# A graph network on one Trainium2 core: fourteen unused products behind each macro's sums in the last layer

## The reference

```python
def _L3_gnn_ref(embeddings, edge_src, edge_dst, edge_val, W1, b1, W2, b2):
    ego_emb = embeddings @ W1.T + b1
    messages = edge_val[:, None] * embeddings[edge_src]
    neighbor_emb = jax.ops.segment_sum(messages, edge_dst, num_segments=embeddings.shape[0])
    interaction_emb = neighbor_emb * embeddings
    side_emb = (neighbor_emb + interaction_emb) @ W2.T + b2
    out = ego_emb + side_emb
    out = jnp.where(out >= 0, out, LEAKY_SLOPE * out)
    norm = jnp.sqrt(jnp.sum(out * out, axis=1, keepdims=True))
    return out / jnp.maximum(norm, EPS)
```

## Time and profile before

| | us |
|---|---|
| median of 3 runs (lowest to highest) | 10351.05 (10349.84 to 10352.02) |
| the profiled execution: its own time | 10342.15 |
| its span | 10340.4 |
| PE busy in the span | 6354.5 |
| POOL busy in the span | 6020.4 |
| DVE busy in the span | 5876.1 |
| mean granted clock of TensorE, of full speed | 0.764 |

### The profile page before, as it was taken

One profiled execution on the slowest core, in us unless ns is written; L12 is line 12 of the kernel. 1 busy time (PEld: TensorE's weight loads), 2 busy tenths in 40 slices (PEclk: granted clock), 3 DMA queues, 4 the chain that ended last, 5 costly groups with the idle time before them and its releaser, 6 DMA issues. The chain is left out here.

```text
span 10340.4 us, 122988 instructions
## 1 busy us (share of the span) xinstructions
PE 6354.5 (61%) x27682; PEld 3894.0 (38%) x27683; DVE 5876.1 (57%) x14147; ACT 2475.6 (24%) x7368; POOL 6020.4 (58%) x5616
## 2 busy tenths in 40 slices
PE   2111255555555555589999947888888885444443
PEld 0011133333333333344444434555555553333332
DVE  4100255555555555468888846888888885222224
ACT  0000133333333333123333312333333331000000
POOL 4777555555556655157877814555555552666661
PEclk6555566666667766589999958999999996676666
DMA  1000132333233333123323513333333342333352
GB/s 60 2 11 10 47 85 79 84 86 84 81 83 86 90 84 83 26 70 85 84 84 85 82 19 89 107 105 105 106 107 105 105 106 59 91 91 91 89 86 34
DMA packets 412331, 792.27 MB, mean 77 GB/s; under 512 B 198946, under 2 KB 228364, under 8 KB 411660
## 3 DMA queue, kind: packets, MB, share of 16 engines
q0 software_dynamic: 284160, 726.76, 27.6%
q1 hardware_dynamic: 128140, 65.15, 2.2%
HBM read 751.30 MB, written 40.22 MB: 77 GB/s over the span
## 5 line engine op out<-in xcount | busy, mean ns | idle before, releaser
L1756 POOL DMA_INDIRECT gat<-y,rec_sb_s x908 | 1189.9, 1310 | 350.6 <-issue 296.8
L495 POOL DMA_INDIRECT rec_s<-wts,rows x784 | 772.2, 985 | 985.8 <-ACT rows L467 774.3
L1521 DVE TENSOR_REDUCE small<-ps 128x2 f32<-128x1024 f32 x900 | 1093.0, 1223 | 305.0 <-PE ps L1389 245.1
L2036 POOL DMA_INDIRECT gat<-x,work x920 | 874.3, 950 | 516.0 <-issue 284.7
L1328 POOL DMA_INDIRECT gat<-kv,rec_sb_s x916 | 914.3, 998 | 420.1 <-issue 314.2
L885 POOL DMA_INDIRECT gat<-kv,rec_sb_d x912 | 938.9, 1029 | 326.1 <-issue 276.4
L2050 PE MATMUL ps<-gat,oh 128*128 128x256 f32 x1792 | 601.2, 507 | 770.4 <-issue 484.6
L434 POOL DMA_INDIRECT rec_d<-small x784 | 809.7, 1033 | 352.0 <-issue 262.4
L1797 PE MATMUL ps<-big,oh 128*128 128x512 f32 x1792 | 964.2, 637 | 0.0
L2050 PEld LDWEIGHTS ps<-gat,oh 128*128 128x128 f32 x1792 | 452.2, 260 | 919.7 <-issue 789.1
L1338 POOL TENSOR_TENSOR big<-gat,big 128x1024 f32<-128x1024 f32 x225 | 442.5, 1967 | 598.5 <-ACT big L1459 596.4
(11 more groups left out here) (282 smaller groups left out, 13414.9 us busy)
## 6 DMA issues: line engine op xcount, KB each, us to landing
gat<-x,work POOLq DMA_INDIRECT x920
gat<-kv,rec_sb_s POOLq DMA_INDIRECT x916
gat<-kv,rec_sb_d POOLq DMA_INDIRECT x912
rec_sb_s<-rec_s SPq DMA_DIRECT2D x456, 32.0 KB, 1.9
gat<-y,rec_sb_s POOLq DMA_INDIRECT x908
kv<-big SPq DMA_DIRECT2D x52, 256.0 KB, 2.0
rec_d<-small POOLq DMA_INDIRECT x784
rec_s<-wts,rows POOLq DMA_INDIRECT x784
```

The lines of the kernel that those rows point to most:

```text
L495: e.indirect_dma_start(out=recs["s"], out_offset=bass.IndirectOffsetOnAxis(ap=pr[:, t:t + 1], axis=0), in_=rr[:, t, :], in_offset=None).th ...
L1521: V.tensor_reduce(mx[:, 2 * pair:2 * pair + 2], psH[pair % 2], AX.X, ALU.max).then_inc(s_hr, 1)
L1756: e.indirect_dma_start(out=rows_y[m.u][:, q, :], out_offset=None, in_=y1, in_offset=bass.IndirectOffsetOnAxis(ap=r_sb[:, m.u, q, 0:1].bitc ...
L2036: e.indirect_dma_start(out=to[m.u][:, q, :], out_offset=None, in_=x3, in_offset=bass.IndirectOffsetOnAxis(ap=r_sb[:, m.u, q, 0:1].bitcast( ...
```

## The change

Behind the four products of a macro, and after the one that signals `sum`, TensorE gets fourteen products whose result nobody reads: the identity (bf16 view) times 512 columns of the features (bf16 view), into PSUM bank 0. They wait for nothing and signal nothing. 224 macros make 3,136 such products, each with its weight load. Nothing else is changed.

```diff
                     last = T.matmul(ps[:, 5 + m.v, 0:D], oh[:, m.off % U, q, :], to[m.u][:, q, :],
                                     start=(q == 0), stop=(q == Q - 1))
                 last.then_inc(s["sum"], 1)
+                for _ in range(14):
+                    T.matmul(ps[:, 0, :], top(ident[:, :]), top(x_sb[:, 0:2, :]),
+                             start=True, stop=True)
 
             def dve_a(e, m):
```

## The result

The changed kernel takes 10393.73 us (median of 6 runs, 10372.61 to 10398.35) against 10351.53 us of the kernel before (6 runs): ratio 1.0045, 95% interval 1.0034 to 1.0056, 42 us slower. Forecast were 10369 us, a range of 10160 to 10440, and 0.35 for slower, as much as for no change. The time lies in that wide range, but 4 us above the forecast's own range, 10345 to 10390.

The account below looks back on a forecast made before the run. GpSimd's gathers, stopped by late sums, were taken to bound the last loop. Other costs 0; cycles at 5.86 us a macro, 0.08 more x 230, gave +18 us: 10360, plus 9 for the median, 10369 us; range 10160 to 10440.

Parts of the forecast that it names:

- The bound: Last layer's edge loop: GpSimd's 920 gathers set the end, 1330.3 us, with 172 us of stops waiting for ScalarE's record copy.
- Rival A: Last layer's loop: TensorE's pauses cause late signals and work cures it; 10170 us, chance 0.22, plus 0.08 for half a cure.
- The argument from the start of layer 1: Against pauses as cause: TensorE busy 13.1 of 14 us, yet products reached ScalarE 2.3 us after GpSimd's last gather ended.
- The price of the products: On TensorE, fourteen products at 0.216 us cost 3.0 us a macro at full clock; with its sums 4.75 us.
- part 5: End of the loop: GpSimd's 24 extra gathers run after TensorE is done, hiding the last macro's products by some 10 us.
- The cycle: GpSimd from restart to restart: two cycles of four macros to one of six, 5.86 us a macro, +18 us.
- the old kind: GpSimd's cycle of six macros between restarts, 34.7 us, kept if the third sum is signalled in time; all such give 0.
- its release: Moment a held third sum was signalled within GpSimd's stream, 10.0, 10.7 or 12.2 us after a restart; caught one in three.
- two released at T, two since: If the third sum misses, GpSimd has four macros from restart T: 20.0 us of gathers, 23.7 with the stop.
- Rival B: TensorE's clock is at half when a cycle starts, second sum held, three macros per 18.5 us; 10438 us, chance 0.15.
- step 3: TensorE's clock rises, lone macros' sums come up to 1.8 us sooner; worth nothing if the sum is then held.
- same: Outcome of no measurable change in kernel time, within 0.2% (21 us): chance 0.27 + 0.08 = 0.35.

Follow-up runs that it names:

- the break: Kernel before with a 128 x 2390 memset on GpSimd ahead of each macro's gathers, gap 2.27 us, on a chip with late sums: 10736.53 us.
- the loop without late sums beside a pausing TensorE, the kernel with four banks: Kernel before with its sums in four PSUM banks instead of two, on a chip without late sums: 9437.65 us, ratio 1.0001.
- the change with four banks: Changed kernel (fourteen products) with its sums in four PSUM banks instead of two, on a chip without late sums: 9435.17 us, ratio 0.9998.
- the other chip: The changed kernel run again on another chip with late sums: 10563.62 us against 10505.54 for the kernel before, ratio 1.0042.
- the run with seven: Changed kernel with seven products a macro instead of fourteen: 10375.89 us against 10347.26 for the kernel before, ratio 1.0032.
- the run that was to separate length from number: Changed kernel with its fourteen products cut to 64 columns, run twice on chips without late sums: 9435.39 and 9438.08 us, ratios 0.9999 and 1.0001.

## Why the prediction was right, and what it missed

**The bound** was right: GpSimd's stops for late sums set the end of the loop, before and after.

**Rival A** (TensorE's pauses cause the late signals, chance 0.22 and 0.08) is out, by three things: the sum held for 6.3 us within an unbroken run of TensorE; the break, which made all sums prompt though TensorE paused before nearly every macro; and the loop without late sums beside a pausing TensorE. The argument from the start of layer 1 had pointed the right way. What is true of it is that fewer sums are late (112 instead of 150) and by less; the time did not follow.

**The price of the products** was nearly right: 4.75 us a macro by the sum, 4.88 measured (9958.32 - 9953.44). Of that 4.88, 3.16 us are products, 0.226 each, not 0.216.

**The end** (part 5): the last product starts at 10163.5, 7.5 us behind the last gather, and not some 10 us ahead of its end. It is hidden all the same, as the next phase starts only at 10177.8.

**The cycle** had the right mechanism with its size off, +18 us against 42 by the medians and 47 by the loops. The term that was mis-sized is the mix of cycles. I took one cycle of six macros (34.7 us) to two of four (23.7 each), 5.86 us a macro. The cycle of four came as forecast, 28 times, 23.89 us on average. But the old kind never came again: the third sum always missed its release. That alone would be the forecast's upper bound, 5.93 us a macro, +34. The other half of the cycles have three macros, 30 times, 18.07 us on average. The common pair is, as above, 23.84 + 18.20 = 42.04 us for seven macros, 6.01 each; x 230 = 1381 us, the loop measured 1376.9.

The step of the sum that these threes break is "two released at T, two since". Two are released at a stop only if the fourth sum of the stream is done by then. I had reckoned that with products TensorE is seldom idle; late in a stream of sixteen it is. From 15.2 us into such a stream there are idle gaps over 0.25 us in the middle of a macro or between products, which wait for nothing (the rows say "issue"): 96 of them in the 28 streams, 100.8 us together, against 11 with 3.7 us in the streams of twelve. They carry the fourth sum past the stop. Neither the kernel before nor the change with four banks on its chip has a single one. Why these matmuls are started late is open.

**Rival B** (chance 0.15) named the cycle of three and its length, 18.5 us, but by another path: it had the second sum held, behind products at half clock. In 27 of the 30 streams of twelve the second sum is done 4.8 to 8.4 us after the restart and is signalled within 0.2 us; what is missing is the sum from the stop. In the three others two copies come with the stop and one in the stream. The one from 9949.97 is of these: its products at 9947.71 take 5.88 us, not 3.16, at a granted clock of 0.52, after TensorE had paused three times from 9942.6 to 9947.3. On the other chip 15 of 41 are of this kind. Half clock is no condition of a cycle of three: the products at 9908.85 run at full clock (3.31 us), and GpSimd issued three macros. So that the threes cost what rival B said is luck of the number.

**The clock** (step 3) came as said, above 0.9 in most of the loop, and was worth nothing.

I gave the forecast and "slower" too little next to "same": by the forecast's own bounds, +34 us was reached without any cycle of three. That the time lies in the stated range is no success of the forecast's sum, as the range was made wide for A and B.

What is shown and what is argued: that the gathers make the sums late, that with four banks and no late sums the products are free, that third sums no longer reach their copy within the stream, and that cycles are of three and four macros is shown. That the third sum misses because the products put 3.16 us ahead of each next sum rests on the ages of the sums in the timelines, in the run with seven above all; the run that was to separate length from number fell on chips that could not tell.

## What to carry to other kernels

Filling an engine's pauses helps only if its own speed is on the path. Here it set nothing: signals were held beside another engine's stream of transfers, and what was put in front of the next sum moved it out of the short prompt stretch. Fewer late signals and a faster clock are no gain by themselves; count what the engine at the end of the chain gets between two of its stops. Before a wait is explained, read when its producer ended and what ended with the wait; a producer that had long been done is not the cause, and giving it more work can only delay what is behind.

## What the runs showed of the hardware

- Two kinds of chips: the same kernel takes 10347 to 10506 us on some and 9437 us on others. In the last loop the difference is 1330.3 against 1154 us, and its rows are the "remote" waits. Most of the rest lies in layer 0, whose gathers of line 885 run for 2969 us in the kernel before and 2327 in the one with four banks. Layer 1 is nearly as long on both: its gathers run 4454.0 to 5960.4 us before, 1506 us, and 1496 us (3720.9 to 5216.6) in the kernel with four banks. Why some chips hold TensorE's signals is open.
- A break between gathers of 0.5 us left the sums late (917.3 us of remote waits); one of 2.27 us, on another chip with late sums, left none of 222 more than 0.2 us late. The value between was run only where no sum is late.
- On the chips with late sums, with the fourteen products, matmuls without a wait start up to 3.6 us late once a stream is 13 us old or more: 139 us of such gaps in the loop, 168 us on the other chip, none in the kernel before and none in the change with four banks where no sum is late.
- A memset between two gathers lies in a gap of 0.30 us that is there anyway: 0.12 us cost nothing of the pace, 0.33 to 0.38 us cost 0.2.
